# GpSimd instead of VectorE subtracts the low part of the MLP's intermediate rows

## What is computed

```
h   = x + mamba2(rmsnorm(x, ln1_w))
mlp = silu(h2 @ gate_w.T) * (h2 @ up_w.T) @ down_w.T        # h2 = rmsnorm(h, ln2_w), 1792 wide inside
x1  = layernorm(x + h + mlp)
x2  = layernorm(x1 + softmax(x1 @ ctx.T) @ ctx)
out = layernorm(x2 + x2 @ W_up.T + (rank-8 product of the expert that has the largest logit))
```

## Time and profile before

| | |
|---|---|
| time, three runs | 433.83, 433.39, 433.07 us; median 433.39 us |
| span of the profiled execution | 432.9 us (the page gives no other time for it) |
| TensorE busy | 417.5 us, 96% of the span |
| VectorE, ScalarE, GpSimd busy | 211.8, 161.4 and 67.6 us |
| tail, from the first down product to the last store | about 290 to 432.9 us |
| GpSimd's last instruction before | starts at 281.45 us |

### The profile page before, as it was taken

How to read it: one execution, slowest core, us unless ns; L and a number is a source line. 1 busy time by engine, 2 the same in 40 slices (tenths; PEclk the granted TensorE clock), 3 DMA queues, 4 the chain that set the end, 5 groups by cost and what they waited for, 6 DMA issues and landing times.

```text
span 432.9 us, 5328 instructions
## 1 busy us (share of the span) xinstructions
PE 417.5 (96%) x1966; PEld 331.7 (77%) x1966; DVE 211.8 (49%) x392; ACT 161.4 (37%) x327; POOL 67.6 (16%) x51
## 2 busy tenths in 40 slices
PE   7999999999999999999999999999999999999984
PEld 2788887766667888888888888888787887887763
DVE  1586996135774431212122222254366576576566
ACT  5636655555653521212121212243232232241221
POOL 2412222344292110101010202020000000000000
PEclk9799999999999999999999999999999999999998
DMA  7610210020020021212121212111101201201001
GB/s 218 246 50 2 91 55 28 22 97 2 0 98 2 2 97 48 97 48 97 48 97 48 97 48 97 48 50 48 48 2 48 74 24 49 73 24 51 24 0 73
DMA packets 10256, 25.67 MB, mean 59 GB/s; under 512 B 1696, under 2 KB 1824, under 8 KB 10240
## 3 DMA queue, kind: packets, MB, share of 16 engines
q1 hardware_dynamic: 9088, 23.36, 16.1%
q10 hardware_dynamic: 1152, 2.10, 1.3%
HBM read 23.36 MB, written 2.10 MB: 59 GB/s over the span
## 4 chain that ended last, share of the span: by engine, by line
PE 88%; DVE 5%; ACT 3%; issue 1%; DMA 1%; SPq 0%; ACTq 0%; DVEq 0%
PE bank L338 25%; PE bank L339 25%; PE bank L340 25%; PE bank L394 2%; PE bank L382 2%; PE bank L546 2%; PE bank L535 1%; DMA rows<-x 1%; PE bank L557 1%; PE bank L403 1%; DVE tmp L1087 1%; PE bank L424 1%; PE bank L349 1%; PE bank L527 1%; PE bank L441 1%
## 5 line engine op out<-in xcount | busy, mean ns | idle before, releaser
L338 PE MATMUL bank<-cols,ringS 128*128 128x512 f32 (+1 forms) x328 | 126.6, 386 | 1.4 <-DVE cols L937 1.3
L340 PE MATMUL bank<-cols,ringS 128*128 128x512 f32 (+1 forms) x328 | 124.5, 380 | 0.0
L339 PE MATMUL bank<-cols,ringS 128*128 128x512 f32 (+1 forms) x328 | 124.5, 380 | 0.0
L338 PEld LDWEIGHTS bank<-cols,ringS 128*128 128x128 f32 x328 | 62.1, 189 | 15.0 <-issue 2.9
L339 PEld LDWEIGHTS bank<-cols,ringS 128*128 128x128 f32 x328 | 62.1, 189 | 11.8 <-issue 0.5
L340 PEld LDWEIGHTS bank<-cols,ringS 128*128 128x128 f32 x328 | 61.9, 189 | 11.6
L1054 DVE TENSOR_TENSOR big<-tmp,bank 128x512 f32 (+1 forms) x28 | 19.3, 688 | 102.2 <-ACT tmp L798 102.2
L338 PE MATMUL bank<-wdS,cols 128*128 128x512 f32 x144 | 61.4, 427 | 0.0
L340 PE MATMUL bank<-wdS,cols 128*128 128x512 f32 x144 | 56.4, 392 | 0.0
L339 PE MATMUL bank<-wdS,cols 128*128 128x512 f32 x144 | 56.2, 390 | 0.0
L798 ACT ACTIVATE tmp<-bank 128x512 f32<-128x512 f32 x28 | 16.8, 598 | 105.6 <-PE bank L340 105.6
(11 more groups left out here) (134 smaller groups left out, 513.2 us busy)
## 6 DMA issues: line engine op xcount, KB each, us to landing
raw<-wstream SPq DMA_DIRECT2D x31, 512.0 KB, 3.2
rows<-x SPq DMA_DIRECT2D x8, 256.0 KB, 4.6
big<-ctxT SPq DMA_DIRECT2D x8, 256.0 KB, 2.6
big<-ctx SPq DMA_DIRECT2D x8, 256.0 KB, 2.9
out<-tmp ACTq DMA_DIRECT2D x8, 256.0 KB, 2.0
big<-ln_w SPq DMA_DIRECT2D x2, 256.0 KB, 5.4
big<-lora_b SPq DMA_DIRECT2D x3, 64.0 KB
ga<-gate_lora SPq DMA_DIRECT2D x1, 72.0 KB
```

The costliest lines, as they stand in the source:

```text
L338: pe.matmul(ps, a_hi, b_lo, start=first, stop=False)
L339: pe.matmul(ps, a_hi, b_hi, start=False, stop=False)
L340: return pe.matmul(ps, a_lo, b_hi, start=False, stop=last)
```

## The change

The subtraction for tiles 1 to 7 leaves VectorE's tail. GpSimd gets the same seven subtractions of 128x1792, after its loop, each behind a wait for `hid_hi` of its tile. The dummy `tail(0, ...)` of VectorE, which did nothing but the split, becomes a wait for the last intermediate rows. Operands, buffers and counts of the semaphores are the same.

```diff
                 pool.tensor_tensor(wdS_t[:, bass.ds(j * CH + NM * D, CH)], raw[:, 0, :],
                                    wdS_t[:, bass.ds(j * CH, CH)].bitcast(F32), ALU.subtract).then_inc(w_lo, 1)
+
+            for t in range(1, B):
+                pool.wait_ge(hid_hi, t + 1)
+                pool.tensor_tensor(hidS[:, t % 2, 1, :], big[:, bass.ts(t, NM * P)],
+                                   hidS[:, t % 2, 0, :].bitcast(F32), ALU.subtract).then_inc(hid_lo, 1)
 ...
-            def split_hid(t, par):
-                v.wait_ge(hid_hi, t + 1)
-                v.tensor_tensor(hidS[:, par, 1, :], big[:, bass.ds(t * (NM * P), NM * P)],
-                                hidS[:, par, 0, :].bitcast(F32), ALU.subtract).then_inc(hid_lo, 1)
-
 ...
-            def tail(t, par, a=True, f=True, g=True, split=True, first_g=False):
+            def tail(t, par, a=True, f=True, g=True, first_g=False):
 ...
                 if a:
                     row_max(t - 1)
-                if split:
-                    split_hid(t + 1, 1 - par)
                 if f:
                     route(t - 2)
 ...
             v.wait_ge(zm_clear, 1)
-            tail(0, 0, a=False, f=False, g=False)
+            v.wait_ge(hid_ok, 2 * NM)
             tail(1, 1, f=False, g=False)
```

## The result

| | before | changed |
|---|---|---|
| median | 433.61 us (433.07 to 434.41, 4 runs) | 451.27 us (451.05 to 451.51, 4 runs) |
| ratio | | 1.0408, 95% interval 1.0395 to 1.0421 |
| span of the profiled execution | 432.9 us | 449.5 us |
| VectorE, GpSimd busy | 211.8, 67.6 us | 212.0, 95.6 us |

A forecast was written before the change was run, and what follows sets the result against it. The prediction took TensorE as the bound, with 0.46 us of slack ahead of `base`. Holding of 11.6 us plus clock falls of 6.8 us made 18.4 us, so 433.4 became 451.8 us, range 442 to 455.

The forecast's parts named there:

- The bound and the slack: TensorE bounds the kernel without gaps in steady tails; L1138 and L1140 have 0.46 us of slack ahead of `base`.
- What is removed, 0: Seven VectorE subtractions of 2.02 us between `row_max` and `route`; TensorE never waited for them, so worth 0.
- GpSimd's duration: Each GpSimd subtraction of 128x1792 takes 4.05 us, estimated from the times for 512 and 1024 elements.
- The start: GpSimd begins its subtraction 0.12 us after ScalarE's copy of the high part ends.
- The copy is held: VectorE's one-input copy L1138, before L1140 and `base`, waits for GpSimd's instruction to end: about 3.5 us instead of 0.43.
- The unknown with two ends: Whether copy L1138 runs free or held under GpSimd: holding sums to 9.2 or 11.6 us; held was taken.
- The holding, 11.6 us: `base` starts late behind held L1138 and L1140: 2.57 us in each of tails 3 to 6, 1.28 in tail 2.
- The clock, four falls at 1.7 us: After TensorE's pauses in tails 3 to 6, 3.4 us at half speed, 1.7 us lost each, 6.8 us together.
- Against the span: Adding 18.4 us to the earlier profiled execution's span of 432.9 us gives 451.3 us.

The follow-up runs named there:

- the run with 512 elements: Changed kernel with GpSimd subtracting only the first 512 elements of each tile and VectorE the other 1280 in its old place: 433.64 us.
- With 1024: Changed kernel with GpSimd subtracting the first 1024 elements of each tile and VectorE the other 768 in its old place: 436.85 us.
- the removal alone: Kernel before with VectorE's seven subtractions left out and nothing in their place: 433.65 us, ratio 0.9993.
- The memset: Kernel before with seven GpSimd memsets of 128x3072 on a dead buffer added, started when the high part is there: 437.87 us.
- work in the pauses: Changed kernel with nine matmuls, results thrown away, ahead of base's wait for its operand in tails 3 to 6: 444.79 us.
- the idle run with two inputs: Kernel before with seven GpSimd subtractions of two different inputs into a dead buffer added, nothing waiting for them: 451.33 us.

## Why the prediction was right

By its steps, against a forecast of 451.8 us with 442 to 455:

- **The bound and the slack.** Confirmed by the run with 512 elements: the copy late by about 0.22 us cost nothing. With 1024 the forecast by the same slack was 437.0, measured 436.85. One reading is off and changes nothing: by the earlier trace rows the full clock begins in the third slice, not the second, which has 7.
- **What is removed, 0.** Measured 0 within 0.2% by the removal alone.
- **GpSimd's duration**, 4.05 us from two shorter lengths: 3.99 to 4.04. The start, 0.12 behind the high part: 0.08.
- **The copy is held.** The unknown with two ends was settled as taken: L1138 has 3.35 us, L1140 its 0.69. The memset shows what does it: GpSimd's writes are enough to hold it. Both kinds agree with the Trainium skill, SBUF — State Buffer, section "Who interferes with whom": copies, casts and tensor-scalar operations can take the pair of ports shared with GpSimd, and a second SBUF input contends only with a GpSimd operation that reads.
- **The holding, 11.6 us.** With work in the pauses 11.2 us are left of the loss (444.79 - 433.61), or 10.4 against the runs of the kernel before beside that one. Tail 2 alone: from its high part's copy to tail 3's it is 18.9 us instead of 17.6, 1.3 as worked out.
- **The clock, four falls at 1.7 us.** Four, of 3.3 to 3.4 us at 1.2 GHz, so 1.6 to 1.7 us lost each; the run with work in the pause gives back 6.5 us where 6.8 was expected. So both terms came out slightly under their forecast, and no large error hides behind another.
- **Against the span.** The tails are longer by 17.8 us (GpSimd's starts in tails 3 to 6 are 20.45 to 20.48 us apart instead of 16.34, four times 4.13, and 1.3 in tail 2), but the spans of the two profiled executions differ by 16.6 only, because the changed one reached tail 0 1.1 us earlier, with a shorter stretch at low clock (0.74 granted from 9.5 to 16.0 us, where the earlier trace rows has 0.50). That start varies between executions and is no part of the change. The medians, 17.7 us apart, agree with the tails.

What was less sure than it read: that a pause is followed by a fall. It held for pauses of 2.3 to 2.4 us (four of four here, and four of four in the idle run with two inputs). None followed the pauses of up to 1.0 us under the memset; at 1.5 us it was three of four.

## What to carry to other kernels

Moving work to GpSimd isn't moving it away from VectorE: read VectorE's instructions in the stretch where GpSimd would run, mark those with two SBUF inputs and the copies and tensor-scalar operations between SBUF tensors, and take each as doing its work only from the end of GpSimd's instruction on (0.14 to 0.21 us before the end of its record in these rows), however small it is. Then compare with the slack of what waits for them; a piece that fits the slack is free, one that doesn't costs the difference in every round, and a matrix engine that pauses long enough (2.3 us here) pays a second time in clock. If GpSimd must work beside it, cut its instruction, since what is held is held for one instruction, and start the pieces by VectorE's own semaphores.

## What the runs showed of the hardware that was not expected

- GpSimd's 128x1792 subtraction takes 3.17 us with one buffer as both inputs and output, 4.0 us with two different inputs.
- The holding works the other way too. In the idle version with two inputs, tile 1's GpSimd subtraction began 0.13 us behind VectorE's and has 5.81 us instead of 4.0; less 4.0 it began its work at 296.08, when VectorE's ended (296.17):

```profile
294.14 2.03 DVE L1090 TENSOR_TENSOR cols<-big,cols 128x1792 fp32r<-128x1792 f32 x1 [1.86 <-ACT cols L839]
294.27 5.81 POOL L333 TENSOR_TENSOR raw<-wdS 128x1792 f32<-128x1792 f32 x1 [11.51 <-ACT cols L839]
```

- Behind a pause of 1.5 us in an otherwise dense stream the clock fell in three tails of four, each fall costing about 1.5 us of stage (19.6 against 18.1 us), though the pauses were alike (1.46 to 1.54 us; the spared one had 1.54). Why one was spared stays open.
